# The second layer's expert loop with its down products cut into pieces of 128 and 64 rows

## The reference

```python
logits = x @ router_w                                   # 256 -> E = 32 experts
probs = softmax(logits)
topk_w, topk_idx = top_k(probs, 4)                      # 4 experts a token
topk_w = topk_w / sum(topk_w)
g = einsum('th,ehi->tei', x, w_gate)                    # hidden size I = 192
u = einsum('th,ehi->tei', x, w_up)
act = silu(g) * u
eo = einsum('tei,eih->teh', act, w_down)                # 192 -> 256
routed = einsum('te,teh->th', combine, eo)
out = routed + sigmoid(x @ sh_gate_w) * shared_expert(x)
```

## Time and profile before

| what | value |
|---|---|
| median of 3 runs | 1324.27 |
| lowest and highest run | 1318.24, 1328.66 |
| profiled execution, its span | 1315.1 |
| TensorE busy in the span | 1243.0 (95%) |
| DVE, ACT, POOL busy | 751.1, 670.4, 700.1 |
| loop in question, from SP's first load to the last down product's end | about 1057 to 1279 |

### The profile page before, as it was taken

One profiled execution on the slowest core, in us unless ns is written; L12 is line 12 of the kernel. 1 busy time (PEld: TensorE's weight loads), 2 busy tenths in 40 slices (PEclk: granted clock), 3 DMA queues, 4 the chain that ended last, 5 costly groups with the idle time before them and its releaser, 6 DMA issues. The chain is left out here.

```text
span 1315.1 us, 25746 instructions
## 1 busy us (share of the span) xinstructions
PE 1243.0 (95%) x8970; PEld 943.9 (72%) x8970; DVE 751.1 (57%) x1590; ACT 670.4 (51%) x1511; POOL 700.1 (53%) x717
## 2 busy tenths in 40 slices
PE   4999897999999999999999989999799989999986
PEld 2677656888888888888888876776546655555544
DVE  6788774444444454554444436777685355656644
ACT  2877754544545555555455436666331145555543
POOL 5565205666566555555566453332038647777750
PEclk9999998999999999999999998999899999999998
DMA  7334333444444444444555458100400167777758
GB/s 256 53 58 62 58 143 112 109 105 107 105 104 108 107 104 97 89 91 105 112 112 113 116 124 295 36 6 2 151 11 1 32 186 235 240 234 233 233 151 319
DMA packets 144149, 161.69 MB, mean 123 GB/s; under 512 B 79141, under 2 KB 104363, under 8 KB 142768
## 3 DMA queue, kind: packets, MB, share of 16 engines
q1 hardware_dynamic: 109776, 106.23, 26.4%
q0 software_dynamic: 32256, 52.46, 19.0%
q10 hardware_dynamic: 2016, 1.71, 0.4%
HBM read 122.60 MB, written 39.85 MB: 124 GB/s over the span
## 5 line engine op out<-in xcount | busy, mean ns | idle before, releaser
L1402 POOL DMA_INDIRECT x_dram<-e_y,rows x128 | 217.4, 1699 | 191.0 <-ACT e_y L1511 165.7
L1498 ACT CAST e_hidden_hi<-e_hid 128x512 fp32r<-128x512 f32 x128 | 79.5, 621 | 161.4 <-DVE e_hid L1546 161.4
L1546 DVE TENSOR_TENSOR e_hid<-e_sg,bank 128x512 f32<-128x512 f32 x128 | 88.0, 688 | 128.4 <-PE bank L1437 94.8
L1437 PE MATMUL bank<-e_xg_hi,e_w_hi 128*128 128x512 f32 x512 | 158.9, 392 | 2.0 <-issue 2.0
L1340 POOL DMA_INDIRECT spare<-xn_dram,rows x128 | 124.9, 976 | 65.5 <-issue 38.4
L1437 PE MATMUL bank<-e_xg_hi,e_w_lo 128*128 128x512 f32 x512 | 158.3, 390 | 0.0
L1437 PE MATMUL bank<-e_xg_lo,e_w_hi 128*128 128x512 f32 x512 | 158.2, 390 | 0.0
L1549 DVE TENSOR_TENSOR e_hidden_lo<-e_hid,e_hidden_hi 128x512 fp32r<-128x512 f32 x128 | 88.6, 692 | 88.0 <-ACT e_hidden_hi L1498 88.0
L1511 ACT ACTIVATE e_y<-bank,shares 128x256 f32<-128x256 f32 x128 | 60.8, 475 | 105.3 <-PE bank L1450 105.0
L2088 PE MATMUL bank<-w,e_xT 128*64 128x384 f32 x320 | 110.0, 486 | 2.2 <-DVE e_wt L2194 1.7
L1437 PEld LDWEIGHTS bank<-e_xg_hi,e_w_lo 128*128 128x128 f32 x512 | 96.7, 189 | 20.3
(11 more groups left out here) (344 smaller groups left out, 2717.0 us busy)
## 6 DMA issues: line engine op xcount, KB each, us to landing
w<-in_L_ffn_w SPq DMA_DIRECT2D x48, 512.0 KB, 5.4
wgu<-in_L_gate_up SPq DMA_DIRECT2D x8, 1536.0 KB, 8.7
V<-in_L_down SPq DMA_DIRECT2D x52, 192.0 KB
kT<-in_L_down SPq DMA_DIRECT2D x52, 192.0 KB
kT<-ys_dram SPq DMA_DIRECT2D x4, 1024.0 KB, 9.0
b_wq<-in_L_down SPq DMA_DIRECT2D x14, 192.0 KB
b_wv<-in_L_down SPq DMA_DIRECT2D x14, 192.0 KB
b_wo<-in_L_down SPq DMA_DIRECT2D x14, 192.0 KB
```

The source lines that it names most:

```text
L1402: nc.gpsimd.indirect_dma_start(out=x_dram[:, :], out_offset=bass.IndirectOffsetOnAxis(ap=rows[:, e, q:q + 1], axis=0), in_=y[q][:, :], in_ ...
L1437: last = nc.tensor.matmul(bank[f % 2][:, :], w[:, k * F0 + f * 128:k * F0 + (f + 1) * 128], x[:, k, h * SLOTS:(h + 1) * SLOTS], start=(w, ...
L1498: nc.scalar.copy(hidden[0][:, f, :], hid[f % 2][:, :]).then_inc(hi_sb, 1)
L1546: nc.vector.tensor_tensor(hid[f % 2][:, :], sg[f % 2][:, :], U_BANK[f % 2][:, :], ALU.mult).then_inc(hid_sb, 1)
```

## The change

The down weights, 192 rows by 256 for each expert, are no longer cut in 96 and 96 rows but in 128 and 64. Of the two pairs of a trip (s = 0, 1), pair 0 has its rows 0 to 127 as the main piece and 128 to 191 as the small one; pair 1 has rows 64 to 191 as the main piece and 0 to 63 as the small one. `hid` of the two pairs stands side by side, 128 x 384, so that three transposes of 128 columns turn it: the middle one holds the two small pieces, pair 0's on partitions 0 to 63, pair 1's on 64 to 127. One ACT copy of 128 x 384 takes the place of two of 96 x 256. `turn_hidden`, `take_hidden` and `down` now serve two pairs in a call. Each pair's result is released after its small piece, which stands behind both main pieces. SP loads the main and the small piece of an expert by two DMAs. The weights are given to the kernel as they are, without the two halves side by side.

```diff
-FH = F1 // 2
+FM = F1 - 128
...
+        wd_main = [[[down_slots[3 * g + u][:, s * D:(s + 1) * D] for u in range(2)] for s in range(2)] for g in range(NDOWN // 2)]
+        wd_more = [[down_slots[3 * g + 2][:, u * D:(u + 1) * D] for u in range(2)] for g in range(NDOWN // 2)]
...
-        hid = [sb(f"hid{v}", [PT, F1]) for v in range(4)]
-        hidT = [sb(f"hidT{v}", [FH, 2, PT]) for v in range(2)]
+        hid = [sb(f"hid{v}", [PT, 2 * F1]) for v in range(2)]
+        hidT = sb("hidT", [128, 3 * PT])
...
-        XT, GU, HT, Y = r.banks[0:2], r.banks[2:4], r.banks[4:6], r.banks[6:8]
+        XT, GU, HT, Y = r.banks[0:2], r.banks[2:4], r.banks[4], r.banks[6:8]
         def half(u):
             return slice(u * TT, (u + 1) * TT)
+
+        MAIN_ROWS = (slice(0, 128), slice(FM, F1))
+        MORE_ROWS = (slice(128, F1), slice(0, FM))
+        MORE_AT = (slice(0, FM), slice(128 - FM, 128))
+        MAIN_T, MORE_T = (0, 2 * PT), PT
...
         @block.sync
         def _(sp):
             def load_down(t):
+                g, s = t // 2 % (NDOWN // 2), t % 2
                 for u in range(2):
                     e = sp.value_load(tile_expert[0:1, u, t:t + 1], min_val=0, max_val=E1 - 1)
-                    sp.dma_start(wd[t % NDOWN][u][:, :, :].rearrange("p k n -> p (k n)"),
-                                 a["L1_down"][bass.ds(e, 1), :, :].rearrange("o p n -> p (o n)")).then_inc(wd_in[t % NDOWN], 16)
+                    sp.dma_start(wd_main[g][s][u], a["L1_down"][bass.ds(e, 1), MAIN_ROWS[s], :].rearrange("o p n -> p (o n)")
+                                 ).then_inc(wd_in[t % NDOWN], 16)
+                    sp.dma_start(wd_more[g][u][MORE_AT[s], :], a["L1_down"][bass.ds(e, 1), MORE_ROWS[s], :]
+                                 .rearrange("o p n -> p (o n)")).then_inc(wd_in[t % NDOWN], 16)
...
             def turn_hidden(t):
-                pe.wait_ge(hid_sb, t + 1)
-                for m in range(2):
-                    last = nc.tensor.transpose(HT[t % 2][0:FH, m * PT:(m + 1) * PT], hid[t % 4][:, m * FH:(m + 1) * FH],
-                                               r.ident[:, :])
+                pe.wait_ge(hid_sb, t + 2)
+                for n in range(3):
+                    last = nc.tensor.transpose(HT[:, n * PT:(n + 1) * PT], hid[t // 2 % 2][:, n * 128:(n + 1) * 128], r.ident[:, :])
                 last.then_inc(ht_ps, 1)
             def down(t):
-                pe.wait_ge(wd_in[t % NDOWN], (t // NDOWN + 1) * 32)
-                pe.wait_ge(ht_sb, t + 1)
-                if t >= 2:
-                    pe.wait_ge(y_sb, t - 1)
-                for m in range(2):
+                g = t // 2 % (NDOWN // 2)
+                pe.wait_ge(ht_sb, t // 2 + 1)
+                for s in range(2):
+                    pe.wait_ge(wd_in[(t + s) % NDOWN], ((t + s) // NDOWN + 1) * 64)
+                    if t >= 2:
+                        pe.wait_ge(y_sb, t + s - 1)
                     for u in range(2):
-                        last = nc.tensor.matmul(Y[t % 2][half(u), 0:D], hidT[t % 2][:, m, half(u)], wd[t % NDOWN][u][:, m, :],
-                                                start=m == 0, stop=m == 1)
-                last.then_inc(y_ps, 1)
+                        tokens = slice(MAIN_T[s] + u * TT, MAIN_T[s] + (u + 1) * TT)
+                        nc.tensor.matmul(Y[s][half(u), 0:D], hidT[:, tokens], wd_main[g][s][u], start=True, stop=False)
+                for s in range(2):
+                    for u in range(2):
+                        tokens = slice(MORE_T + u * TT, MORE_T + (u + 1) * TT)
+                        last = nc.tensor.matmul(Y[s][half(u), 0:D], hidT[MORE_AT[s], tokens], wd_more[g][u][MORE_AT[s], :],
+                                                start=False, stop=True)
+                    last.then_inc(y_ps, 1)
...
                     up(t + 2)
                     up(t + 3)
                 turn_hidden(t)
-                turn_hidden(t + 1)
                 if t + 4 < PAIRS:
                     turn_over(t + 4)
                     turn_over(t + 5)
                 down(t)
-                down(t + 1)
...
             def take_hidden(t):
-                act.wait_ge(ht_ps, t + 1)
-                nc.scalar.copy(hidT[t % 2][:, :, :].rearrange("p m t -> p (m t)"), HT[t % 2][0:FH, 0:2 * PT]
-                               ).then_inc(ht_sb, 1)
+                act.wait_ge(ht_ps, t // 2 + 1)
+                nc.scalar.copy(hidT[:, :], HT[:, 0:3 * PT]).then_inc(ht_sb, 1)
...
                     gate(t + 2)
                     gate(t + 3)
                 take_hidden(t)
-                take_hidden(t + 1)
                 if t + 4 < PAIRS:
                     take_weights(t + 4)
                     take_weights(t + 5)
...
             def gated(t):
                 dve.wait_ge(sg_sb, t + 1)
-                nc.vector.tensor_tensor(hid[t % 4][:, :], sg[t % 2][:, :], GU[t % 2][:, F1:2 * F1], ALU.mult
-                                        ).then_inc(hid_sb, 1)
+                nc.vector.tensor_tensor(hid[t // 2 % 2][:, t % 2 * F1:(t % 2 + 1) * F1], sg[t % 2][:, :], GU[t % 2][:, F1:2 * F1],
+                                        ALU.mult).then_inc(hid_sb, 1)
...
-        "L1_down": np.asarray(inputs["L1_ffn_w_down"]).reshape(E1, 2, FH, D).transpose(0, 2, 1, 3).reshape(E1, FH, 2 * D),
+        "L1_down": inputs["L1_ffn_w_down"],
```

More of the change, by code:

```diff
@@ L1988, in experts1_phase @@
         wt = [[w_raw[v][:, 0:KD * 2 * F1], sb(f"wt{v}_1", [128, KD * 2 * F1])] for v in range(NBUF)]
-        wd = [[t[0:FH, :, :] for t in pair] for pair in (pair[0:2], pair[2:4])]
+        down_slots = [t[:, :, :].rearrange("p k n -> p (k n)") for t in pair]
         NY = 4
@@ L1996, in experts1_phase @@
         rest = idle[1][:, whole:2 * whole]
-        wd += [[rest[0:FH, u * 2 * D:(u + 1) * 2 * D].rearrange("p (k n) -> p k n", k=2) for u in range(2)]]
-        wd += [[p[0:FH, u, 0:2, :] for u in range(2)] for p in picked[1:NDOWN - NBUF + 1]]
+        down_slots += [rest[:, u * 2 * D:(u + 1) * 2 * D] for u in range(2)]
+        down_slots += [picked[n][:, u, 0:2, :].rearrange("p k d -> p (k d)") for n, u in ((1, 0), (1, 1), (2, 0))]
+        wd_main = [[[down_slots[3 * g + u][:, s * D:(s + 1) * D] for u in range(2)] for s in range(2)] for g in range(NDOWN // 2)]
+        wd_more = [[down_slots[3 * g + 2][:, u * D:(u + 1) * D] for u in range(2)] for g in range(NDOWN // 2)]
         xT = [sb(f"xT{v}", [128, KD, PT]) for v in range(2)]
         sg = [sb(f"sg{v}", [PT, F1]) for v in range(2)]
-        hid = [sb(f"hid{v}", [PT, F1]) for v in range(4)]
-        hidT = [sb(f"hidT{v}", [FH, 2, PT]) for v in range(2)]
+        hid = [sb(f"hid{v}", [PT, 2 * F1]) for v in range(2)]
+        hidT = sb("hidT", [128, 3 * PT])
         yt = [t[:, KD * 2 * F1:] for t in w_raw] + [rest[:, v * D:(v + 1) * D] for v in range(4, 8)] + [sb("yt", [128, D])]
```

## The result

The changed kernel takes 1408.7 us (median of 4 runs, 1407.2 to 1411.4), beside 1326.5 for the kernel before in the same session: 1.065 times as long, with a 95% interval of 1.059 to 1.070. The direction was as predicted. The size was not: 1357 was predicted, and 1408.7 is 29 us above the range's upper end.

A forecast was written before the change was run, and what follows sets the result against it. TensorE bounds the loop before, SP after: 160 x (1.096 + 0.47) = 250.6 us; with landing and last products +32.8 us, span 1347.9, plus 9.2 to the median gives 1357 us. Range 1338 to 1380.

The forecast's parts named there:

- Rival A: SP's loop loads: the second issue is nearly free, so TensorE's gain shows; 1310 us, chance 0.06.
- Rival C: DMA engines: each packet costs the same whatever its size, +55 us, 1379 us; chance 0.03.
- I take 0.47 us: SP's stream: each load's added issue costs 0.47 us, between 0.38 and 0.59, register instruction included.
- pairs 1.8 us apart: Sign in SP's timeline: issue pairs 1.8 us apart, instead of about 1.57, would mean the issue was mis-sized.
- The mean of a load: SP's work per load before the added issue: taken as 1.096 us, between 1.075 and 1.117.
- The landing: Loop's end: the last 64 KB of down weights land 3.0 us after SP's last issue.
- the last products: TensorE at the loop's end: three steps of 0.214 and a record of 0.38, 1.0 us after landing.
- the gain on TensorE: TensorE's loop trip: shorter by 0.15 to 0.52 us, middle 0.34, 14 us over 40 trips, hidden by waiting for weights.
- The four pieces in two rounds and the shorter transposes: TensorE's trip: row halves run at once, saving 0.43 us; three hidden transposes instead of four save 0.09.
- the two changes of shape: TensorE's trip: the 64 x 64 pieces add two array-shape changes, costing 0 to 0.20 us together.
- the wait for the one longer copy: TensorE's trip: waiting for the single 384-column copy of the hidden tile costs 0 to 0.17 us.
- rival B: Loop: no change, the issue is cheap but POOL's 5.38 us a trip holds TensorE (1320 us), or SP ends near parity; chance 0.07.

The follow-up runs named there:

- the quarter transfers: The changed kernel with both issues kept, but from the seventh pair on moving 32 and 16 rows instead of 128 and 64: 1381.4 us (one run).
- the fixed-expert run: The kernel before, each load in two issues of 96 rows of 1 KB, the second from a fixed expert without register instruction: 1369.4 us (two runs).
- the first experiment: The kernel before, TensorE untouched, each load cut into two issues of 96 rows of 1 KB behind one register load: 1371.9 us, ratio 1.039.
- the run without the second issue: The changed kernel without the 64-row load from the seventh pair on: 1328.3 us (10 runs), ratio 1.003.

## Why the prediction was right or wrong

**Right: the bound and the mechanism.** SP bounds the loop: its wait for slots fell from 32.9 to 0.7 us, TensorE waits ahead of the 128-row products for DMAs of the down weights, and splitting the issues in the otherwise unchanged kernel is enough to slow it by 45 us. Rival A (the second issue nearly free) falls with that. The Trainium skill, DMA: Bandwidth & Descriptors, section Issuing engines are not separate DMA queues, calls the sequencer's time to start a DMA usually small relative to the DMA. Here it is not small: the two issues of a load take SP 0.35 + 0.48 = 0.83 us, while its 192 KB take the 16 engines about 0.68 us (an estimate, by the 3.46 us per MB below). Rival C falls by the quarter transfers. So does its premise: SP's queue moved 29.29 MB with 36.2% of 280 us after and 25.80 MB with 47.0% of 180 us before, 3.46 and 3.28 us of all engines per MB, 5.5% more for the narrower rows (4% was estimated). The row of the DMA view after, 1080 to 1360, with the columns of the earlier trace rows:

```profile
q1 hardware_dynamic: 33341, 29.29, 36.2%
```

**Wrong: the size of the added issue.** The step that failed is "I take 0.47 us", with its bounds of 0.38 and 0.59 and "the register instruction is inside these bounds". What was added is 1.80 - 1.07 = 0.73 us at an undisturbed step, above the upper bound. The 0.47 is right for an issue of 96 rows (1.54 - 1.07, the fixed-expert run). On top come 0.16 us because it is one of 64 rows (0.48 against 0.32), 0.04 for the register instruction, 0.03 for the first issue with 128 rows in place of 96 (0.35 against 0.32) and 0.03 for the longer way to the next issue (0.78 against 1.07 - 0.32 = 0.75). The prediction took the price from loads of other forms and read the spread of the earlier trace rows as a bound; the form itself was a price of its own that no row of before showed. The prediction's own sign for this mistake, pairs 1.8 us apart, is what SP's rows show.

**Wrong: the steps that take longer.** The mean of a load lay 0.03 above its undisturbed step in the sum (1.096 against 1.07), and 0.08 above it in the run (1.879 against 1.80): 38 of 159 steps are longer, 14 us together. They do not fall at random. In the changed kernel, the quarter transfers, the two issues in the other order and the first experiment, whose loads have the same number of SP's instructions, the step behind load 14, 29, 43, 57, 71, 86, 100, 114, 128, 142 and 157 (counted from 0) is longer each time, by 0.26 to 0.74 us, though their bytes and order differ; in the fixed-expert run, with one instruction fewer in a load, eight of these eleven places are undisturbed. So part of the extra goes with the place in SP's stream of instructions, about 5 of the 14 us in the changed kernel. What SP waits for there was not found; the profile names nothing.

Together 1.879 - 1.566 = 0.313 us a load, x 160 = 50.1 us. The landing was shorter (1365.41 to 1367.14 = 1.73 us, where 3.0 was taken) and the last products longer (1367.14 to 1368.19 + 1.13 = 2.18, where 1.0 was taken), which nearly cancels. The span has 7.3 us more from the stages ahead and 2.8 behind the loop: 1347.9 + 50.1 + 7.3 + 2.8 = 1408.1, beside 1408.0. The runs' median is 0.7 above this span instead of 9.2: the profile before is of an execution shorter than the median, the profile after is not.

**Wrong, and hidden: the gain on TensorE.** -0.34 us a trip was forecast, and -0.15 to -0.52 allowed; it is -0.02 (5.45 against 5.47). The four pieces in two rounds and the shorter transposes were right: -0.43 and -0.09. Against them stand, in the trip without second issues above: from the last main round to the pieces 1182.44 - 1182.12 = 0.32 in place of 0.21, and from the pieces to `up` 0.59 in place of two rounds of 0.214, together 0.27 for the two changes of shape (0 to 0.20 was allowed); the first step of `up`, 1183.40 - 1183.03 = 0.37 in place of 0.32; and the down products begin 1.11 us after the hidden transposes where 1.01 - 0.09 = 0.92 would be, 0.19 for the wait for the one longer copy, which ends at 1180.89 + 0.48 = 1181.37 (0 to 0.17 was allowed). 0.27 + 0.05 + 0.19 = 0.51, which eats the 0.52. Both upper ends were passed, and the first step of `up` had no term. The Trainium skill, TensorEngine Tiling (Array Packing), section Key Properties, says that a change of the tiling mode drains the engine: the rows agree, with 0.11 us into the 64 x 64 pieces and 0.16 out of them. By that rule the sum was to be taken at its upper waits, -0.15 us a trip; the rows show that even this was too much gain.

So a version in which SP holds nothing up only ties with the kernel before. That the tie comes from TensorE and not from POOL (rival B) is shown by its records, which in such a trip follow each other with no wait but that for ACT's copy. POOL is close behind: in the run without the second issue its four instructions and the idle time ahead of each take 1179.64 to 1185.07 = 5.43 us of the 5.45, so a much shorter trip of TensorE would probably have met POOL; no run tests that.

## What to carry to other kernels

An engine that issues many small loads is a bound like any other: count its instructions, price each by a row of the same form, and ask how much slack the engine has before a load is cut in two, here 32.9 / 160 = 0.2 us a load. When the form is new (rows, width, or what stands between two issues), a bench of a few forms in one run shows its price, while the spread over other forms does not bound it. A better packing of the array pays only what is left after the changes of shape and the longer wait for a bigger copy; where two new shapes appear in each trip, put their cost at its upper end.

## What the runs showed of the hardware

The issue price by form, above, was not expected: 0.48 us for 64 rows, 0.32 to 0.35 for 16, 32, 48, 96 and 128 in the same places, and a longer way to the next load behind 112 + 56. ACT's queue shows the same two prices where it issues half of the loads: 0.35 us for 128 rows and 0.48 for 64 (medians). Without register loads two issues take 1.15 us in place of 1.80, so the register load of the expert's number costs 0.65 us of each step; it stands there for 0.79 us, but the first issue is 0.59 us long without it and 0.35 behind it.

TensorE's clock reacted to the waits. The windows view after, around the trip shown in the first section:

```profile
1174.00:1179.70 5.70, 2.64 (x23) 1.21 (x23) 2.20 (x5) 2.36 (x4) 3.16 (x3) 1.00 0.61 196
1179.70:1182.90 3.20, 3.20 (x14) 1.25 (x12) 0.76 (x2) 0.28 (x1) 1.52 (x2) 0.50 0.49 148
1183.00:1188.00 5.00, 4.87 (x39) 2.40 (x37) 3.19 (x8) 2.38 (x4) 2.35 (x3) 0.99 0.63 182
```

After 5.70 us in which it was busy for 2.64, TensorE ran at a granted clock of 0.50 (its lower level, 1.2 GHz) for 3.2 us although it was busy throughout, and then at 0.99. At the lower level a step of `up` takes 1180.43 - 1179.74 = 0.69 us for the first and about 0.64 for the next ones in place of 0.37 and 0.32 (the run without the second issue). In the middle of the loop that hides behind SP (the mean trip is four of SP's loads); at the loop's end it shows. From 1367.10 to 1369.40 the granted clock was 0.50, and the last pair's first step was 0.48 (1367.14 to 1367.62), where it is 0.27 at the upper level (1181.42 to 1181.69 in the run without the second issue), and of the 2.18 us named above about 0.9 are due to it (0.27 + 0.32 + 0.66 = 1.25 by the rows at the upper level). Before, with no waits, the clock was 1.00 over the window of the earlier trace rows.
